# Issuing half of the stacked query and key loads from ScalarE in a two-layer attention kernel

## What is computed

```python
q, k = rope(q), rope(k)                      # 16 heads of 16 features
scores = einsum('bqhd,bkhd->bhqk', q, k) / sqrt(16)
scores = where(causal (and within the window in the first layer), scores, -inf)
attn = einsum('bhqk,bkhd->bqhd', softmax(scores), v)
```

## Time and profile before

| | before |
|---|---|
| median of three runs | 1862.9 us |
| the profiled execution | 1861.47 us |
| its span, first to last instruction | 1859.7 us |
| mean granted TensorE clock | 0.975 |
| TensorE busy | 1733.4 us, 93% |
| VectorE busy | 1016.1 us, 55% |
| ScalarE busy | 886.3 us, 48% |
| GpSimd busy | 835.7 us, 45% |
| loads from `split`, all on SP's queue | 372 of 128 KB, 24 of 64 KB |

### The profile page before, as it was taken

The page is one execution under the profiler, slowest core; times in us unless marked ns, Lnnn a source line. Parts: engine busy times, 40 slices in busy tenths (PEclk is TensorE's granted clock), DMA queues, the critical chain, the costliest instruction groups (busy, mean ns, idle before and its releaser), DMA issues. The chain is left out here.

```text
span 1859.7 us, 34083 instructions
## 1 busy us (share of the span) xinstructions
PE 1733.4 (93%) x11399; PEld 1130.5 (61%) x11399; DVE 1016.1 (55%) x2357; ACT 886.3 (48%) x1877; POOL 835.7 (45%) x1295
## 2 busy tenths in 40 slices
PE   6899998999999899999999999999879999999992
PEld 5666765665476656557765654544647766667771
DVE  4557677868567985857698677885401100011014
ACT  2455463657756365675637467566322222212223
POOL 4674663522368683137868323455432211221223
PEclk9999999999999999999999999999889999999996
DMA  6725337132343313234512214242033233332116
GB/s 211 95 71 68 44 103 131 19 52 92 47 71 75 87 24 47 70 50 69 91 29 36 35 47 70 44 76 71 29 122 85 40 65 83 90 88 62 20 23 192
DMA packets 106055, 131.27 MB, mean 71 GB/s; under 512 B 15882, under 2 KB 77467, under 8 KB 105744
## 3 DMA queue, kind: packets, MB, share of 16 engines
q1 hardware_dynamic: 89488, 117.08, 29.6%
q0 software_dynamic: 14336, 11.41, 4.5%
q10 hardware_dynamic: 2064, 0.61, 0.2%
HBM read 53.96 MB, written 38.01 MB: 49 GB/s over the span
## 5 line engine op out<-in xcount | busy, mean ns | idle before, releaser
L1114 ACT ACTIVATE b_probs<-b_psum 128x512 f32<-128x512 f32 (+3 forms) x896 | 417.8, 546 | 184.3 <-PE b_psum L975 182.6
L1378 DVE TENSOR_REDUCE b_mneg<-b_psum 128x2 f32<-128x384 f32 (+5 forms) x608 | 331.9, 591 | 88.5 <-PE b_psum L962 87.2
L1477 POOL TENSOR_SCALAR_AFFINE_SELECT b_probs<-b_probs 128x512 f32<-128x512 f32 (+1 forms) x400 | 239.3, 610 | 284.7 <-ACT b_probs L1114 273.9
L962 PE MATMUL b_psum<-b_qk 96*128 96x192 bf16 (+4 forms) x1280 | 292.5, 294 | 3.1 <-DVE b_mhalf L1378 1.1
L975 PE MATMUL b_psum<-b_qk 99*128 99x192 bf16 (+5 forms) x1344 | 261.5, 289 | 11.3 <-DMA b_qk<-b_mrow 7.0
L1711 POOL DMA_INDIRECT before_last_norm<-b_ye,b_ids x64 | 99.1, 1549 | 347.6 <-DMA before_last_norm<-b_ye,b_ids 195.2
L1808 ACT ACTIVATE b_hid<-b_psum,b_b 128x512 f32<-128x512 f32 (+1 forms) x136 | 90.0, 662 | 336.1 <-PE b_psum L1751 336.1
L1852 DVE TENSOR_TENSOR b_ye<-b_psum,b_qk 128x512 f32<-128x512 f32 (+1 forms) x33 | 22.3, 675 | 388.5 <-PE b_psum L1759 388.5
L989 PE MATMUL b_psum<-b_probs,b_v 128*32 128x192 f32 (+4 forms) x2688 | 197.6, 414 | 3.8 <-POOL b_probs L1477 3.0
L962 PEld LDWEIGHTS b_psum<-b_qk 96*128 96x128 bf16 x1280 | 122.8, 99 | 93.4 <-issue 24.7
L1378 DVE TENSOR_REDUCE b_mhalf<-b_psum 128x1 f32<-128x512 f32 x256 | 165.0, 680 | 15.0 <-PE b_psum L962 14.3
(11 more groups left out here) (227 smaller groups left out, 2772.9 us busy)
## 6 DMA issues: line engine op xcount, KB each, us to landing
b_qk<-b_split SPq DMA_DIRECT2D x372, 128.0 KB, 5.5
slot_rows<-before_last_norm SPq DMA_DIRECT2D x32, 256.0 KB, 3.9
b_qk<-in_W SPq DMA_DIRECT2D x8, 1024.0 KB, 7.5
b_xg<-slot_rows SPq DMA_DIRECT2D x16, 512.0 KB, 9.6
b_w<-in_W SPq DMA_DIRECT2D x8, 1024.0 KB
before_last_norm<-b_early SPq DMA_DIRECT2D x4, 1024.0 KB, 4.4
b_o<-before_last_norm SPq DMA_DIRECT2D x4, 1024.0 KB, 5.5
before_last_norm<-b_o SPq DMA_DIRECT2D x4, 1024.0 KB, 4.5
```

Source lines behind the costliest of these rows:

```text
L962: ins = pe.matmul(out[:, i, :], q[0:KS, h, P * t:P * t + P], q[0:KS, HG + h, a:e], start=not last, stop=True, skip_group_check=True)
L1114: act.activation(probs_of((g, h2, t), a, e)[:, heads[0]:heads[-1] + 1, :], bank, ACT.Exp, scale=SCALE).then_inc(s.exp_done, 1)
L1378: dve.tensor_reduce(out, in_bank(("max",) + x[1:], heads, e - a), AX.X, ALU.max, negate=True).then_inc(s.max_read, 1)
L1477: ins = pool.affine_select(out=block, in_=block, pattern=[[0, HG], [1 if ahead else -1, z - y]], compare_op=ALU.is_ge, fill=none, base=y - ...
```

## The change

The loads of keys (a = 1, six a group) become a step kind of their own, `load_k`, on ScalarE; those of queries (a = 0) stay on SP. The instruction that a load makes, its waits and its semaphore are the same; they move into a helper that takes the engine. The scheduler's figures change with it: a load costs SP 0.69 us and ScalarE 0.55 us, whole or half, and lands after 5.1 us. Since `load` and `load_k` are two kinds, each with an order of its own, the scheduler may run both side by side, and it orders all engines anew by these figures.

```diff
-    LANDING = {"load": 4.5, "spread": 2.2, ...
+    LANDING = {"load": 5.1, "load_k": 5.1, "spread": 2.2, ...
...
                 for a in range(2):
                     for slot in SLOTS_OF[a][part]:
-                        add(("load", g, a, slot, y), "SP", 0.55 if y is not None else 1.05, (kind, g // 2, q), last)
+                        if a:
+                            add(("load_k", g, a, slot, y), "ACT", 0.55, (kind, g // 2, q), last)
+                        else:
+                            add(("load", g, a, slot, y), "SP", 0.69, (kind, g // 2, q), last)
...
-                        y = (("load", 0, 1, 2, t // 4) if g == 0 else ("load", g, 1, 2, None))
+                        y = (("load_k", 0, 1, 2, t // 4) if g == 0 else ("load_k", g, 1, 2, None))
...
+    def load_part(eng, g, a, slot, y):
+
+        part = [slot in slots for slots in SLOTS_OF[a]].index(True)
+        eng.wait_ge((s.high_done, s.mid_done, s.low_done)[part], 4 * (g // 2) + (4 if y is None else 2 * y + 2))
+        if g >= RING:
+            eng.wait_ge(s.exp_done, order[("power",) + plan.last_piece(g - RING, 1)] + 1)
+        cols = slice(0, T) if y is None else slice(BANK * y, BANK * y + BANK)
+        eng.dma_start(u.qk[g % RING][HD * slot:HD * slot + HD, HG * a:HG * a + HG, cols],
+                     u.split[HG * HD * (g % 2):HG * HD * (g % 2 + 1), a, part, cols]
+                     ).then_inc(loaded[g % RING if g else RING + y], 16)
...
             for x in plan.program["ACT"]:
                 kind = x[0]
-                if kind in LAYER_KINDS:
+                if kind == "load_k":
+                    load_part(act, *x[1:])
+                elif kind in LAYER_KINDS:
```

More of the change, by code:

```diff
@@ L107 @@
     LATE = {"PE": 0.2, "DVE": 0.14, "ACT": 0.14, "POOL": 0.1}
-    LANDING = {"load": 4.5, "spread": 2.2, "source": 4.0, "x3_in": 3.0, "x3_out": 3.0, "x4_out": 3.0, "put": 2.5, "zeros": 6.0, "expert": 8.0}
+    LANDING = {"load": 5.1, "load_k": 5.1, "spread": 2.2, "source": 4.0, "x3_in": 3.0, "x3_out": 3.0, "x4_out": 3.0, "put": 2.5, "zeros": 6.0, "expert": 8.0}
     def takes(self, x):
@@ L350, in prep @@
                 add(("proj", j, t), "PE", 1.29, rows,
-                    name("load", 2 * j - 1, 1, 5, None) if t == 0 else None,
+                    name("load_k", 2 * j - 1, 1, 5, None) if t == 0 else None, name("load", 2 * j - 1, 0, 5, None) if t == 0 else None,
                     self.final_values(2 * j - 3, 1) if j >= 2 else None)
@@ L359, in prep @@
                     add(("turn", j, q), "PE", 0.435, ("add", j, t))
-                    add(("high", j, q), "ACT", 0.52, ("turn", j, q), *[name("load", g, a, 5, None if g else 1)
+                    add(("high", j, q), "ACT", 0.52, ("turn", j, q), *[name("load_k" if a else "load", g, a, 5, None if g else 1)
                                                                       for g in (2 * j - 2, 2 * j - 1) if j for a in range(2)])
@@ L753, in _ @@
                 elif kind == "load":
[L754 to L762, removed]
+                    load_part(sp, *x[1:])
                 elif kind == "spread":
```

## The result

The changed kernel takes 1993.75 us (median of three runs, 1989.03 to 1996.51) where the kernel before took 1862.9: a ratio of 1.07, interval 1.0666 to 1.0733. The forecast was 1881, with a range up to 1900. The direction was right and the size was not: 131 us were lost where 19 were forecast, and only 15 of them by the wait that the forecast went by. Most of the rest came by a term that it had as a gain, so that the direction came out right is in part luck.

A forecast was written before the change was run, and what follows sets the result against it. The prediction took TensorE's own list as the bound. It added -6 us for the start and the maxima to +25 for the new order, +19 in all: 1881 us, range 1848 to 1900, the forecast's own 1868 to 1900.

The forecast's parts named there:

- the wait that the forecast went by: TensorE's first products in eight groups would wait 3.2 us each for loads from `split`, 25 us in all.
- a term that it had as a gain: TensorE's 7.0 us of waits for the maxima sent by SP were to shrink by 2 us.
- The bound: In the attention, TensorE's own list sets the time; a change gains only in its pauses, 40.75 of 1050 us.
- The transfers' pace: In load bursts, a whole 128 KB load is limited by its transfer, 1.03 us at 127 GB/s, not its issue.
- faster rival: Transfers keep up with two queues, groups land sooner, no 3.2 us waits appear; about 1853 us, chance 0.32.
- The order built for other figures: New figures move eight groups' first products 7.9 us forward, ahead of their loads: +25 us, ends 0 and 46.
- The maxima: At the start, maxima on SP stand behind fewer loads: 2 us gained of TensorE's 7.0 us of waits.
- Clock and slack: Half-speed clock after TensorE's pauses costs time, other pauses shrink; the two were set against each other.
- ScalarE's issues at 0: ScalarE's 198 added issues, 119 us, lift it to about 70% busy; TensorE's list covers them, price 0.
- rival that put them at 40 us: ScalarE's issues and the wait for `low` hold back exponentials in eight groups: 40 less 6, 1895 us; chance 0.07.
- wait for `low`: ScalarE's added wait for GpSimd's work, with exponentials queued behind it: taken as 0, between 0 and 11.4 us.
- The start, -6: First group's half loads issue on two queues: 2 us gained at TensorE's first wait, 4 by the second; with maxima -6.

The follow-up runs named there:

- e3: The changed kernel with the scheduler's landing time for the maxima that SP sends set to 9.0 us instead of 2.2; 1949.86 us, ratio 1.047.
- e1: The changed kernel with scheduler figures paced to the transfers (2.1 us for two loads, half loads 1.1, landing 4.5); 1906.44 us, ratio 1.0228 to the kernel before.
- e5: The order of e1, but SP issues all loads and ScalarE none; 1885.79 us, ratio 1.0132 to the kernel before.
- e2: The changed kernel's order, but SP issues each key load behind its query load and ScalarE none; 2023.11 us, ratio 1.0863 to the kernel before.
- e6: The kernel before with its own figures, but ScalarE issues the twelve key half loads of group 0 only; 1859.24 us, ratio 0.9992.
- e4: The kernel before, all loads on SP, but ScalarE sends the maxima on its own queue behind the copy that makes them; 1900.32 us, ratio 1.0212.

## Why the prediction was right and wrong, point by point

- **The bound, right.** TensorE's list sets the time, and all that was lost is its pauses and its clock. ScalarE's share did not rise (busy 896.4 us), as issuing is not counted in it.
- **The transfers' pace, right.** With two queues the stretches of the pause shown above move 116 to 143 GB/s at a DMA share over 1, where the burst of the earlier trace rows moved 127. The Trainium skill, "DMA: Bandwidth & Descriptors", "Issuing engines are not separate DMA queues", has DMAs of all issuing engines run on the same 16 engines; the trace agrees. The faster rival (1853) falls with these rates: no stretch shown reaches the 162 GB/s that it counted on, and no run shows that loads which land in different partitions add up.
- **The order built for other figures, right in kind.** 25 us of new waits for loads were forecast, 15.1 came: the first products of four of the eight groups (8, 12, 20 and 24) wait 1.6 to 6.1 us and begin 15.7 to 16.9 us after their first load, where the working had 15.0 for the transfers. The two waits at the start fell from 4.5 to 2.1 us. With the maxima cured (e3) there are 43.5 us of waits for loads, 39 more than before, where 46 was the upper end. It fits this that the larger wait hid the rest in the changed kernel, but e3's order is another one, so it is not shown.
- **The maxima: the step that failed.** The prediction put it so: "The maxima on SP stand behind fewer loads: of their 7.0 us I take 2", as a gain. It looked at SP's line of issues alone. The maxima share the DMA engines with the backlog of loads that the same text had worked out, and are planned at 2.2 us; they cost 69 us more, not 2 less. Its own row of TensorE's waits named them as the larger of the two, 7.0 against 4.5.
- **Clock and slack: the second.** "I set the two against each other": the clock cost 38 us of busy time, since long pauses leave the lower level behind them (0.50 after 256 us), and no slack came back: the pauses for all else grew by 12 us.
- **ScalarE's issues at 0, wrong.** With a paced order they cost 18 us (e1 against e5), and the start shows one place where they stand in front of TensorE. In the changed kernel TensorE waits 30.4 us for ScalarE's work, 15.0 in the same order without these issues (e2); what they cost in time there is not told apart, since e2 loses more on DMAs. The rival that put them at 40 us had the mechanism in part, with waits for exponentials of 13.7 us where 1.7 stood. The wait for `low` holds ScalarE's exponentials for 2.0 us in the whole run (last of their idle times, by line), near the 0 that was taken; what it holds in front of other work, as among the ten loads of the start, that line does not count:

```profile
L1122 ACT ACTIVATE b_probs<-b_psum 128x512 f32<-128x512 f32 (+3 forms) x896 | 427.0, 538 | 344.8 <-PE b_psum L981 327.7 <-issue 10.5 <-POOL b_split L1507 2.0
```

- **The start, -6, too much.** The first products gained 1.4 and 2.1 us in place of 2 and 4; in e6, where the two come as early, the time is that of before (0.9992, 0.9978 to 1.0005).

The sum as it came out: maxima +69, loads +13, other pauses +12 (11 of them for ScalarE), busy time +38, together 132 by the spans.

## What to carry to other kernels

A figure that a scheduler holds for a DMA should be the time that the shared DMA engines need for it, not what it costs the engine that issues it; splitting the issue over two engines did not halve it here. When transfers are packed more closely than they move, look for the small DMAs issued among them, on whatever queue: they wait in the backlog, and an engine that comes to them too early pays. A long pause of TensorE is to be counted twice, once as a wait and once at the lower clock behind it. And an issue on an engine that computes has a price of its own: 18 us for 198 of them in e1's order.

## What the runs showed of the hardware that was not expected

A DMA of 12 KB that lands in 2.2 us in the median took 11.2 us until TensorE could use it, with 21 loads of 128 KB around it on two queues. A queue of its own did not spare it: in e4, with all loads on the other queue, one took 11.3 us. In the scheduler, the figure need not be far off: with a load planned at 0.8, 1.05 and 1.15 us, the kernel takes 1881, 1860 and 1872 us, though the last step may be the chance of a new order.
